# The first maxima of attention: ScalarE copies half of the pieces in bf16, VectorE joins them, and the first scores move ahead of four pieces

## What is computed

```
qkv = einsum('bsi,oi->bso', x, w_qkv) + b_qkv          # 16 heads, 16 wide each
attn = einsum('bhqd,bhkd->bhqk', q, k) * scale
attn = softmax(attn, axis=-1)                           # over 1024 keys
vals = einsum('bhqk,bhkd->bhqd', attn, v)
out  = einsum('bse,oe->bso', vals, w_o) + b_o
```

## Time and profile before

| what | us |
|---|---|
| median of 3 runs | 1400.64 (1399.13 to 1400.97) |
| the profiled execution, its own time | 1401.21 |
| its span in the trace | 1399.5 |
| TensorE busy in it | 1341.7 (96%) |
| VectorE busy in it | 1124.4 (80%) |
| ScalarE busy in it | 737.6 (53%) |

### The profile page before, as it was taken

One profiled execution on the slowest core, in us unless ns is written; L12 is line 12 of the kernel. 1 busy time (PEld: TensorE's weight loads), 2 busy tenths in 40 slices (PEclk: granted clock), 3 DMA queues, 4 the chain that ended last, 5 costly groups with the idle time before them and its releaser, 6 DMA issues.

```text
span 1399.5 us, 30567 instructions
## 1 busy us (share of the span) xinstructions
PE 1341.7 (96%) x8199; PEld 673.0 (48%) x8200; DVE 1124.4 (80%) x2816; ACT 737.6 (53%) x1127; POOL 607.6 (43%) x791
## 2 busy tenths in 40 slices
PE   6999999999999999999999999999999999999995
PEld 4562222333323323333233233668788888887542
DVE  6879999999999999999999992665566666666488
ACT  3551777767676767676767777123333333333100
POOL 1300122514634536445346366347755555555300
PEclk9996999999999999999999999999999999999998
DMA  6778665337446534463465446857766656656698
GB/s 201 227 231 199 139 166 114 66 77 162 86 110 142 127 89 107 119 163 84 101 152 150 91 127 213 252 171 229 227 200 198 201 170 188 181 166 181 243 339 338
DMA packets 264906, 235.31 MB, mean 168 GB/s; under 512 B 159286, under 2 KB 230470, under 8 KB 264684
## 3 DMA queue, kind: packets, MB, share of 16 engines
q1 hardware_dynamic: 237452, 159.23, 44.3%
q0 software_dynamic: 21872, 68.07, 13.8%
q10 hardware_dynamic: 5488, 6.82, 1.5%
HBM read 129.78 MB, written 104.22 MB: 167 GB/s over the span
## 4 chain that ended last, share of the span: by engine, by line
PE 71%; DVE 14%; DMA 3%; issue 2%; ACT 1%; POOL 1%; SPq 0%; DVEq 0%; POOLq 0%
PE psO L1250 15%; PE psE L1237 13%; PE ex_psGU L1758 13%; PE psM L1227 10%; DVE piece_max L1124 9%; PE ex_psY L1773 7%; PE ex_psX L1747 3%; PE psM L578 2%; DMA wide<-results 2%; PE ex_psA L1767 2%; PE psGU L1571 1%; PE co_psS L2027 1%; PE psM L597 1%; DVE wide L1988 1%; PE psX L1585 1%
## 5 line engine op out<-in xcount | busy, mean ns | idle before, releaser
L1124 DVE TENSOR_REDUCE piece_max<-psM 128x1 f32<-128x512 f32 x1024 | 642.6, 682 | 24.5 <-PE psM L1227 21.3
L1191 ACT ACTIVATE wide<-psE 128x1024 f32<-128x1024 f32 x512 | 497.2, 1021 | 203.4 <-PE psE L1237 201.1
L1227 PE MATMUL psM<-wide 48*128 48x512 bf16 x1024 | 323.5, 394 | 14.5 <-DVE piece_max L1124 12.5
L1237 PE MATMUL psE<-wide 49*128 49x512 bf16 (+1 forms) x2048 | 329.3, 380 | 0.3
L1839 POOL DMA_INDIRECT results<-vals_inv,places x223 | 214.0, 960 | 153.8 <-DVE vals_inv L1825 91.0
L1250 PE MATMUL psO<-wide 128*32 128x512 f32 x2048 | 273.9, 607 | 0.6 <-ACT wide L1191 0.6
L1227 PEld LDWEIGHTS psM<-wide 48*128 48x128 bf16 x1024 | 78.0, 93 | 342.7 <-DVE piece_max L1124 278.4
L1758 PE MATMUL ex_psGU<-wide,ex_xT 128*128 x892 | 232.3, 383 | 0.9 <-ACT ex_xT L1790 0.6
L1237 PEld LDWEIGHTS psE<-wide 49*128 49x128 bf16 (+1 forms) x2048 | 117.7, 95 | 89.2 <-issue 8.5
L1758 PEld LDWEIGHTS ex_psGU<-wide,ex_xT 128*128 128x128 f32 x892 | 152.0, 190 | 17.4 <-issue 4.4
L1790 ACT ACTIVATE ex_xT<-ex_psX 128x256 f32<-128x256 f32 x223 | 85.3, 383 | 121.7 <-PE ex_psX L1747 120.8
(11 more groups left out here) (280 smaller groups left out, 1234.2 us busy)
## 6 DMA issues: line engine op xcount, KB each, us to landing
wide<-qk_parts SPq DMA_DIRECT2D x384, 64.0 KB
wide<-results SPq DMA_DIRECT2D x16, 1536.0 KB, 9.4
rows<-lists SPq DMA_DIRECT2D x112, 160.0 KB
h2Ts<-lists SPq DMA_DIRECT2D x111, 160.0 KB
qk_parts<-parts SPq DMA_DIRECT2D x32, 384.0 KB, 2.9
xin<-in_x_dram SPq DMA_DIRECT2D x16, 512.0 KB, 4.1
wide<-in_guT_dram SPq DMA_DIRECT2D x3, 2560.0 KB
lists<-pad_row SPq DMA_DIRECT2D x32, 160.0 KB
```

The source lines that it names most:

```text
L1124: v.tensor_reduce(piece_max[:, qh, (x * PAIRS + h) * KT // QH + qt, kh:kh + 1], bank_of("piece", PIECES * group + n), AX.X, ALU.max, negat ...
L1191: nc.scalar.activation(probs[:, step % 2, 2 * pair:2 * pair + 2], psE[:, pair], ACT.Exp, scale=HD ** -0.5).then_inc(exp_ok, 1)
L1227: nc.tensor.matmul(bank_of(*user), qa[g][rows, h, qt * P:(qt + 1) * P], ka[g][rows, h, kh * 512:(kh + 1) * 512], start=True, stop=True).th ...
L1237: mm = nc.tensor.matmul(psE[:, pair, x], k[g][part, pair, kt * P:(kt + 1) * P], q[g][part, pair, qh * 512:(qh + 1) * 512], start=(q is qa) ...
```

## The change

Of the first 32 pieces, the sixteen of the first key half (n % 4 < 2) are no longer reduced by VectorE. ScalarE copies each from PSUM into `probs` as bf16 (new semaphore `copied`), and VectorE takes the maxima of eight copies at a time: four elementwise maxima that halve the width (512 to 32) and one reduction, each waiting for the one before (`join_copies`). The first set of eight is joined after piece 27, the second after piece 31. TensorE's waits for a free bank follow whichever engine read it. In the second part, TensorE's first scores (step 0) stand after piece 39, and pieces 40 to 43 between and behind the two pairs; before, they stood after piece 43.

```diff
+            def join_copies(h):
+                dve.wait_ge(copied, COPIES // PAIRS * (h + 1))
+                width = 512
+                while width > 32:
+                    width //= 2
+                    chain.link(v.tensor_tensor(copies[:, h, :, 0:width], copies[:, h, :, 0:width],
+                                               copies[:, h, :, width:2 * width], ALU.max))
+                x_parts = piece_max[:, 0].rearrange("p (x h q) k -> p x h q k", x=2, h=PAIRS)
+                v.tensor_reduce(x_parts[:, :, h, :, 0], copies[:, h, :, 0:width].rearrange("p (q x) n -> p x q n", x=2),
+                                AX.X, ALU.max, negate=True).then_inc(joined, 1)
...
             for n in range(HALF_PIECES):
-                piece_maximum(0, n)
+                if n % 4 >= 2:
+                    piece_maximum(0, n)
+                if n == JOIN:
+                    join_copies(0)
+            join_copies(1)
             dve.wait_ge(env.zeroed, 1)
+            dve.wait_ge(joined, PAIRS)
             finish(0)
...
+            for n in range(HALF_PIECES):
+                if n % 4 < 2:
+                    x, h, qh, qt, kh = piece_at(n)
+                    act.wait_ge(piece_done, n + 1)
+                    nc.scalar.activation(copies[:, h, 2 * qt + x], bank_of("piece", n), ACT.Copy).then_inc(copied, 1)
...
-                if c == "piece":
-                    pe.wait_ge(piece_read, w + 1)
+                if c == "piece" and w >= HALF_PIECES:
+                    pe.wait_ge(piece_read, w + 1 - COPIES)
+                elif c == "piece":
+                    pe.wait_ge(copied if w % 4 < 2 else piece_read, 2 * (w // 4) + w % 2 + 1)
...
-            for n in range(HALF_PIECES + 4 * AHEAD):
+            early = HALF_PIECES + 4 * (AHEAD - 1)
+            for n in range(early):
                 piece(0, n)
+            pe.wait_ge(max_there, 16)
+            for pair in range(2):
+                scores(0, 0, 0, pair)
+                for n in range(2):
+                    piece(0, early + 2 * pair + n)
```

More of the change, by code:

```diff
@@ L809, in attention_phase @@
     PAIRS = HG // 2
+    COPIES = HALF_PIECES // 2
+    JOIN = 27
     NGR = B * NG
@@ L817, in attention_phase @@
         probs = env.wide[:, GPART * NG:].rearrange("p (n h q) -> p n h q", n=2, h=HG)
+        copies = probs[:].rearrange("p n h q -> p (n h q)").bitcast(BF16).rearrange("p (h n q) -> p h n q", h=PAIRS,
+                                                                                    n=COPIES // PAIRS)
         o_sb = sb("o_sb", [P, HD, S // HD], F32)
@@ L831, in attention_phase @@
                                           "max_ready", "max_stored", "max_there", "o_read", "o_stored", "den_stored", "den_in", "divided", "inv_stored", "chain"))
+        copied, joined = env.sem("att_copied"), env.sem("att_joined")
         env.inv_stored = inv_stored
@@ L838, in attention_phase @@
         env.const_in = const_in
+        env.copies = COPIES
         env.spare_in = spare_in
@@ L1129, in finish @@
                 cols = slice(COLS * (k % QH), COLS * (k % QH + 1))
-                dve.wait_ge(piece_read, HALF_PIECES * (k + 1))
+                dve.wait_ge(piece_read, HALF_PIECES * (k + 1) - COPIES)
                 chain.link(v.tensor_tensor(neg_max[:, cols], part[:, :, 0], part[:, :, 1], ALU.min))
@@ L1275, in _ @@
                 g = group % NG
-                if s % KT == 0:
+                if step and s % KT == 0:
                     pe.wait_ge(max_there, 16 * (step // KT + 1))
@@ L1280, in _ @@
                     pe.wait_ge(loaded[to % NG], 16 * LOADS * (to // NG + 1))
-                scores(step, g, s, 0)
+                if step:
+                    scores(step, g, s, 0)
                 if to < NGR:
                     piece(to, first)
-                scores(step, g, s, 1)
+                if step:
+                    scores(step, g, s, 1)
                 if to < NGR:
@@ L1596, in _ @@
             shared_in(1, 0, 0)
-            pe.wait_ge(env.piece_read, 2 * HG * KT * B * NG)
+            pe.wait_ge(env.piece_read, 2 * HG * KT * B * NG - env.copies)
             pe.wait_ge(env.placed_read, LAST)
```

## The result

The changed kernel takes 1404.99 us (median of 12 runs, 1402.22 to 1409.64). Beside it the kernel before took 1401.34 (12 runs, 1399.13 to 1404.70). The ratio is 1.0027, with a 95% interval of 1.0016 to 1.0038: 3.8 us slower, between 2.2 and 5.3. The profiled execution has a span of 1401.0 us.

A forecast was written before the change was run, and what follows sets the result against it. VectorE's reductions bound attention's start until about 131 us, then a TensorE-VectorE loop passes delays on. 1401.21 + 2.6 = 1403.8 profiled, 0.6 above the median, so 1403.2 us; 62% for 1401.8 to 1405.2, full range 1400.0 to 1407.0.

The forecast's parts named there:

- The ring: First 32 pieces: the loop through three PSUM banks takes 1.98 us for four pieces, 0.50 a piece against 0.60 before.
- The joins: VectorE's two joins of copied pieces: 3.2 us each, wholly on the path, 6.4 in all.
- The term that was bounded and not seen: In each join, the first elementwise bf16 maximum of 2048 results: an estimated 1.22 us at double pace.
- The rival of a single pace: Joins take 5.2 us each, 4.0 more ahead of the first scores: +6.6, 1407.2 us; chance 13%.
- The maxima: End of the first 32 pieces: `neg_max` at 133.1 instead of 131.29, 1.8 us later.
- Part two: Scores moved among the pieces: first scores 0.2 us later than before, step 1 begins 2.3 us later.
- VectorE's gaps behind piece 39: Between `neg_max` and step 1, VectorE has two gaps among its 13 reductions, 1.1 us in all.
- The clock: Full clock returns later in time, not earlier in the order of work: +2.6 us, between bounds +1.2 and +4.1.
- The whole time: Whole kernel: 1403.2 us, from +2.6 on the profiled execution, which is 0.6 above the median of 1400.64.
- The rival of a ring that doesn't bind: First 32 pieces: VectorE never waits, `neg_max` at 128.3, step 1 1.3 us earlier, 1399.3 us; chance 13%.

The follow-up runs named there:

- e3: Copies and joins with the old order, first 32 pieces in seven PSUM banks instead of three; ratio to the kernel before 0.9984.
- e7: The kernel before with seven banks for the first 32 pieces and no copies, on another chip; `neg_max` 19.33 us after the first reader.
- e2: The kernel before with only the order changed, step 0's scores after piece 39; ratio to before 0.9999.
- e4: The changed kernel with the first join after piece 15 instead of 27; `neg_max` 21.38 us after the first reader.
- e10: e3 (seven banks, copies) with the change's order of the first scores, after piece 39; ratio to the kernel before 1.0001.
- e11: e3 run again unchanged, on one chip with e10; ratio to the kernel before 0.9987.
- e5: The changed kernel with four PSUM banks instead of three for the first 32 pieces, on another chip; `neg_max` 17.55 us after the first reader.
- e8: e3 with 12 of group 1's 25 loads ahead of the first maxima's store and 13 behind; ratio to the kernel before 1.0022.

## Why the prediction was right

The forecast was 1403.2 us with a range up to 1405.2; 1404.99 lies in it, near its end. Point by point, times again from the first reader:

- *The ring.* 1.98 us for four pieces were worked out, 1.99 are in the trace, with the pause of 0.70 foreseen. e3 to e7 leave no other cause.
- *The joins.* 3.2 us each: the first takes from 125.01 to 128.19, 3.18. The term that was bounded and not seen is settled: the first maximum of 2048 results in bf16 takes 1214 ns, as long as 1024 in f32 (1226). The Trainium skill, "VectorE: DVE Perf Modes", "The perf-mode tier table", had said that two bf16 tensors go at twice the pace and a reduction does not, and the trace agrees: 1214 ns for 2048, and 420 for a reduction of 256 in bf16 as in f32. The rival of a single pace falls.
- *The maxima.* 1.8 later were forecast, 2.05 are there. The 0.25 is most likely the run-in: VectorE's second piece stood 1.04 after the first reader in my reckoning and is at 112.48 - 111.19 = 1.29, where the clock was low already 0.4 us after the first reader, not 1.4. From there on the reckoned and the measured times run side by side (the first join 13.5 and 13.8).
- *Part two.* The first scores were to be 0.2 later than before and are 0.5 later; step 1's 2.3 and are 2.7 (141.91 - 111.19 = 30.72 against 28.06). Most of that is the 0.25 of the maxima. The prediction puts VectorE's gaps behind piece 39 at 1.1 us in all, but that figure doesn't fit its own times: from piece 32 at 133.7 to the end of 44 at 142.2 are 8.5 us, 0.6 more than the 7.87 of before. Measured are 0.6 as well, 0.51 of it ahead of piece 40. e2 measures the order's own share: 0.5 us at step 1.
- *The clock.* Step 1 took 146.09 - 141.91 = 4.2 us, the last 0.4 us of it at full clock: the clock came back 34.5 after the first reader, before 32.1 after it, both times at the end of step 1. +2.6 was taken, +2.5 stands at the end of step 1. That the clock came back there again, and not later, is in part luck. The prediction ties its return to the order of work, and e7 speaks against that, though on its other chip: step 1's scores stand at 28.06 as before, but the clock came back 34.9 after the first reader, 2.3 us behind the end of step 1. In e3 it came back 2.0 behind it. In the changed kernel that would have cost another 0.9 us, an estimate from step 2 of e3 (3.37 against 2.48). The windows of e7 over steps 0 and 1 and over the start of step 2 (the next one, from 146.40 on, has 1.00):

```profile
136.90:144.00 7.10, 7.10 (x34) 2.00 (x33) 5.51 (x9) 3.93 (x4) 0.00 (x0) 0.50 0.72 137
144.10:146.20 2.10, 2.10 (x12) 0.63 (x10) 1.57 (x3) 0.71 (x1) 0.58 (x1) 0.50 1.11 126
```

The Trainium skill, "TensorE: Matmul & The Clock Gate", "What's actually happening", says activity releases the throttle; the rows agree so far as they go (0.50 from shortly behind the first pieces, 1.00 only once the weighted values had begun, in every kernel of the table: at the end of step 1, or in e3 2 us behind it), but TensorE's busy time alone doesn't tell when, as it was 18.00 of 18.00 us at 0.50 in the earlier trace rows, and no run varies this by itself.
- *The whole time.* 1403.2 was forecast from a median of 1400.64 (of 3; the 12 beside the changed kernel have 1401.34), so +2.6 or 0.18%; measured are 0.27%, 0.16 to 0.38. The difference above 2.5 us is within the spread of the executions, and as the trace of before has a drop of the clock in attention that the changed one has not, two traces can't say where it lies. The prediction took 2.8 us as what can be told from no change, and its forecast lay on that border; so does the result, 3.8 with an interval from 2.2 to 5.3.

The rival of a ring that doesn't bind was the right picture for another kernel: e3 shows it, with `neg_max` at 16.15 (16.3 worked out for it) and the store held up by group 1's loads.

## What to carry over

Before a second engine is set to drain a ring, count the loop of one bank: reader's time, plus hand-over, plus the producer's latency to the reader at the clock that holds there. If the ring is short, two readers win little, and what they free is idle time that other work need not be able to fill (e4). Moving a consumer ahead in a stream pays only where the stream's own bound moves with it; here the next step waited for VectorE's piece 44, not for the scores. And when a small transfer comes sooner, look at what stands ahead of it in its queue, and at what stands ahead of the next one once that has been moved.

## What the runs showed of the hardware

- From the start of a matmul of 512 columns to its reader is 0.41 us at the full clock (111.55 to 111.96) and 0.64 to 0.68 at the low one (111.84 to 112.48 in the changed kernel; 142.11 to 142.79). Where a ring binds, this latency stands whole in each turn: 0.64 of the 1.99 us here.
- From the store of 8 KB to the load that waits for it were 2.0 us where the store was issued 6 us behind the last load of a group (before), and 4.6, 4.8 and 6.6 us where it was issued 2 to 3 us behind (e3, e10, e11): the same place in the stream of SyncE, and a spread of 2 us.
- Short stretches at a granted clock of 0.50 occur in the midst of attention with TensorE at work, in one execution and not in the next: one of about 3 us at 492 in before put it back by 1.16 us (2.14 - 0.98).
- The chips differ: on the one of e5 to e8 the kernel before took 1523.8 us against 1401.4, with a mean granted clock of 0.96 against 0.98. How much of the difference is the clock's isn't shown. At the start of attention nothing differs: in e7 `neg_max` stands at 19.33, as on the other chip.
